# Attention reciprocals copied by VectorE shuffles instead of through DRAM, with larger rings in the expert weights' memory

## The chip, the cores and the metric

The kernel runs on one core of one Trainium2 chip. The metric is the device time of one launch in microseconds (us). The kernel before takes 1158.88 us, the median of 3 runs (1156.53 to 1162.4).

## The reference, cut to what matters

`x` is 8 batches of 1024 rows of 128. The block is attention with an adjacency mask, then a mixture of 8 experts.

```python
# attention, after a layer norm of x; H = 4 heads of 32, Nc = 8 chunks of 128 keys
scores = einsum('bhnd,bhjcd->bhnjc', q, kc) / sqrt(32)
scores = clip(scores, -10, 10);  scores = where(mask == 0, -10, scores)
attn = softmax(scores, axis=-1)          # over the 128 keys of one chunk
ctx = einsum('bhnjc,bhjcd->bhnd', attn, vc)
out = layernorm(ctx @ Wo.T + bo + x) * gamma + beta
# experts, after a layer norm: top 2 of 8 by a softmax gate
h = gelu(xf @ w1 + bb1);  y = h @ w2 + bb2;  acc = acc + we[:, None] * y   # for each expert
```

The softmax is over each chunk alone. So every query has 8 denominators a head, one a chunk, and the part of the context from each chunk is multiplied by its own reciprocal before the chunks are added.

## The kernel before, in words

**Attention.** A batch is 16 steps (`STEPS`): 2 halves of 512 queries by 8 chunks of keys. In a step PE computes `scores` of two heads twice (u = 0, 1; L1123), VectorE clips and masks them (`clip`, L822), ScalarE takes the exponential (L621), PE multiplies by `v` (`contexts`, two steps later, L1137) and adds up the denominators (`denominators`, L1150). ScalarE copies the context of the step from PSUM to the ring `ctx_sb` (`ctx_copy`, L597; `RING` = 8 places), and GpSimd multiplies it by `rspread` and adds it to the sum of its half (`normalise`, L408 to L416), `LAG` = 9 steps behind in its list. Between these stand the projections of the next batch and the output projection and layer norm of the last (`post_...`). Each engine has its list in a fixed order, and all waiting is by semaphores.

**The reciprocals.** The denominators of 4 steps (`GROUP`) and 4 heads lie in one PSUM tile of 128 rows by 256: in the 32 rows of a head, row 2j + c holds step j of the group, queries c x 256 to c x 256 + 255. VectorE inverts it once in 4 steps into `rinv` (`invert`, L833). GpSimd needs, for each step, the 512 reciprocals of a head in all its 32 partitions. `spread` on SP's queue makes that copy: it stores `rinv` in DRAM (L335, 128 KB), waits until it has landed, and loads it back with each row repeated over 32 partitions (L341, two transfers of 512 KB, each for two steps). `rspread` has 4 places, and each of the two transfers waits until GpSimd has used the places before (`chunk_added`). The next batch's Q and K go through DRAM on ScalarE's queue (`qk_dram`, then `qstack` and `kstack`, L570 and L583).

**The rest.** SP's list runs in order. It loads x of batch 0, weights, x of batches 1 to 3, and the adjacency; after the mask is made, the expert weights W1 and W2 (L322, L324), into the place of x of batches 4 to 7; and, behind the first `spread` and the split of the weights, x of batches 4 to 7 (`load_x(2)`). VectorE takes the statistics of these in steps 9 to 13 of batch 0 (L795). GpSimd splits W1 and W2 into high and low halves (`split_ffn`, L456 to L460) at the start. After attention VectorE takes statistics of all rows (L946), the gate follows, and from about 755 us the experts: `hidden`, gelu, `second`, with GpSimd at L507.

Of the kernel before, what the change touches and what calls it, by code (L numbers as in the profile page):

```python
# [24 lines left out]
ACT = mybir.ActivationFunctionType  # L25
# [7 lines left out]
P = 128  # L33
# [9 lines left out]
def gnn_moe(nc, x, adj, Wq, bq, Wk, bk, Wv, bv, Wo, bo, gamma, beta, gate_w, gate_b, W1, b1, W2, b2, out):  # L43
# [19 lines left out]
    with ctx:  # L63
# [37 lines left out]
        w_raw = [x1[:, NB - 4 + 2 * i:NB - 2 + 2 * i, :].rearrange("p b n -> p (b n)") for i in range(2)]  # L101
# [16 lines left out]
        rspread = sb("rspread", [P, GROUP, HALF], F32)  # L118
# [15 lines left out]
        hid = ctx_sb[:, :, :].rearrange("p (r k) n -> p r k n", k=KH)  # L134
# [43 lines left out]
        den_dram = nc.dram_tensor("den_dram", (2, P, HALF // 2), F32, kind="Internal").ap()  # L178
# [44 lines left out]
        rinv_stored = sem("rinv_stored")  # L223
        rspread_loaded = [sem(f"rspread_loaded{j}") for j in range(GROUP)]
# [74 lines left out]
        def _(sp):  # L299
# [21 lines left out]
            sp.wait_ge(mask_made, T)  # L321
            sp.dma_start(w_raw[0].rearrange("p (e h) -> p e h", e=E),  # L322
# [3 lines left out]

            def spread(b, i, pairs=range(GROUP // 2)):

                G = GROUPS * b + i
                if pairs[0] == 0:  # L330
                    sp.wait_ge(rinv_ready, G + 1)


                    wait(sp, rspread_loaded[GROUP // 2 - 1], 16 * (G - 1))
                    sp.dma_start(den_dram[i % 2], rinv[:]).then_inc(rinv_stored, 16)  # L335
                    sp.wait_ge(rinv_stored, 16 * G + 16)
                rows = den_dram[i % 2].rearrange("(h m i r) q -> h m i (r q)", h=HEADS, i=GROUP // 2, r=GROUP)
                for j in pairs:

                    wait(sp, chunk_added, GROUP * (G - 1) + 2 * j + 2)  # L340
                    sp.dma_start(rspread[:, 2 * j:2 * j + 2, :],  # L341
                                 rows[:, 0, j:j + 1, :].to_broadcast([HEADS, DH, 2 * HALF])
                                 ).then_inc(rspread_loaded[j], 16)

            def body(b, par=None):
                par = b % 2 if par is None else par
                first, last = isinstance(b, int) and b == 0, isinstance(b, int) and b == LAST
                if not first:
                    spread(b - 1, GROUPS - 1)
                spread(b, 0)  # L350
                if first:

                    sp.wait_ge(ffn_step, 6)
                    load_x(2)
                spread(b, 1)
                spread(b, 2)

            batches(body)
            spread(LAST, GROUPS - 1)

# [12 lines left out]
        def _(pool):  # L373
# [24 lines left out]
            def normalise(b, s):  # L398
# [4 lines left out]
                pool.wait_ge(rspread_loaded[s % GROUP // 2], 16 * (GROUPS * b + s // GROUP + 1))  # L403
                fresh, by = ctx_sb[:, s % RING, :], rspread[:, s % GROUP, :]
# [57 lines left out]
            def body(b, par=None):  # L462
# [3 lines left out]
                for s in range(STEPS):  # L466
                    if s == 0 and not first and not second:
                        post_root(2 * b - 3)
                    if s == 12 and not first:
                        post_root(2 * b - 2)  # L470
                    if s >= LAG:
                        normalise(b, s - LAG)
                    elif not first:
                        normalise(b - 1, s - LAG + STEPS)
                    if s == 5 and not first and not second:
                        post_final(b - 2, 1)
                    if s == 14 and not first:
# [3 lines left out]
                    if s == 0 and first:  # L481
                        split_ffn(0, w1_hi[:, :, :].rearrange("p e h -> p (e h)"),
                                  w1_lo[:, :, :].rearrange("p e h -> p (e h)"))
                    if s == 4 and first:
                        split_ffn(1, w2_hi[:, :, :, :].rearrange("p e k d -> p (e k d)"),
                                  w2_lo[:, :, :, :].rearrange("p e k d -> p (e k d)"))
# [13 lines left out]
            post_final(LAST, 1)  # L500

# [16 lines left out]
        def _(act):  # L518
# [72 lines left out]
            def ctx_copy(b, s):  # L591
# [5 lines left out]
                act.activation(ctx_sb[:, s % RING, :], sum_ps[:, s % 2, :], ACT.Copy).then_inc(ctx_copied, 1)  # L597
# [143 lines left out]
        def _(dve):  # L741
# [85 lines left out]
            def invert(b, i):  # L827
# [57 lines left out]
            def body(b, par=None):  # L885
# [512 lines left out]
```

## Time and profile before

| | |
|---|---|
| median of 3 runs | 1158.88 us |
| the profiled execution | 1162.74 us, span 1160.9 us |
| PE busy | 921.1 us, 79% |
| VectorE busy | 773.1 us, 67% |
| ScalarE busy | 613.8 us, 53% |
| GpSimd busy | 713.5 us, 61% |
| transfers for `rspread` | 64 of 512 KB |
| transfers for `den_dram` | 32 of 128 KB |

The span is the time from the first to the last instruction in the profile; the execution's own time is 1.84 us longer. DVE is VectorE, ACT ScalarE, POOL GpSimd, and SPq and ACTq are the queues that issue transfers. Busy time doesn't count waiting, so a share says nothing by itself of what sets the end; the waits and the chain do.

### The profile page before, as it was taken

What the parts mean: (1) busy time and instruction counts of PE and PEld (TensorE: products, weight loads), DVE (VectorE), ACT (ScalarE), POOL (GpSimd) and SP (SyncE); (2) the same over time, 40 slices, a digit from 0 to 9 for tenths busy, and PEclk for the clock granted to TensorE, in tenths of its full rate; (3) what the DMA queues carried; (4) which work ended last, traced back from release to release, by engine and by line L of the source; (5) the groups of instructions that cost most, each with busy time, mean ns of one, the idle gap of its engine ahead of it and who ended that gap; (6) DMA issues with size and microseconds to landing.
All of it is one profiled execution on the core that took longest, in us unless ns stands there. A gap on an engine that the chain in (4) does not pass through costs nothing.

```text
span 1160.9 us, 23125 instructions
## 1 busy us (share of the span) xinstructions
PE 921.1 (79%) x8456; PEld 450.0 (39%) x8456; DVE 773.1 (67%) x1763; ACT 613.8 (53%) x948; POOL 713.5 (61%) x637
## 2 busy tenths in 40 slices
PE   4582797997877969879689407199999899899997
PEld 2221132231222313212222106056666666666665
DVE  5563897776765838758577386866666566566665
ACT  4561586756747658477566415154444344444443
POOL 2512455666656666667476860057787677777776
PEclk9595899898988979989899755589999999999999
DMA  8544426243262432433522210000000000000000
GB/s 283 132 95 103 106 84 145 73 130 99 84 139 75 130 102 79 120 100 97 134 66 76 77 42 1 0 2 11 19 11 11 12 10 11 21 10 11 10 11 20
DMA packets 42375, 79.59 MB, mean 69 GB/s; under 512 B 3196, under 2 KB 18455, under 8 KB 42263
## 3 DMA queue, kind: packets, MB, share of 16 engines
q1 hardware_dynamic: 28438, 52.92, 14.8%
q10 hardware_dynamic: 13824, 25.17, 9.3%
q8 instruction: 71, 1.16, 0.4%
q14 instruction: 42, 0.34, 0.1%
HBM read 61.30 MB, written 16.78 MB: 67 GB/s over the span
## 4 chain that ended last, share of the span: by engine, by line
DMA 31%; POOL 28%; issue 15%; PE 14%; DVE 9%; ACT 2%; POOLq 1%; ACTq 1%; SPq 1%; DVEq 0%
DMA rspread<-den_dram 14%; POOL prob_ring L507 14%; DMA den_dram<-rinv 9%; POOL ctx_sb L411 5%; POOL ctx_acc L416 4%; DMA x<-in_x 3%; DMA kstack<-qk_dram 2%; PE score_ps L1123 2%; DMA qk_dram<-qk_lo 2%; PE sum_ps L1137 2%; PE side_ps L1150 1%; POOL ctxT L416 1%; POOL x L442 1%; PE sum_ps L1319 1%; DVE limit L946 1%
## 5 line engine op out<-in xcount | busy, mean ns | idle before, releaser
L822 DVE SCALAR_TENSOR_TENSOR prob_ring<-score_ps,limit 128x1024 f32<-128x1024 f32 x256 | 305.7, 1212 | 123.2 <-PE score_ps L1123 122.6
L507 POOL TENSOR_TENSOR prob_ring<-ctx_sb,prob_ring 128x512 f16<-128x512 f32 x256 | 305.5, 1213 | 118.2 <-DVE prob_ring L1013 118.2
L621 ACT ACTIVATE prob_ring<-prob_ring 128x1024 f32<-128x1024 f32 x256 | 262.7, 1052 | 127.3 <-DVE prob_ring L822 97.3
L696 ACT ACTIVATE ctx_sb<-score_ps,vec 128x512 f32<-128x512 f32 x256 | 166.9, 684 | 171.4 <-PE score_ps L1085 171.4
L411 POOL TENSOR_TENSOR ctx_sb<-ctx_sb,rspread 128x512 f32<-128x512 f32 x112 | 142.9, 1276 | 157.4 <-DMA rspread<-den_dram 145.2
L1023 DVE SCALAR_TENSOR_TENSOR prob_ring<-sum_ps,cw_s,prob_ring 128x128 f32<-128x128 f32 x512 | 144.1, 344 | 136.7 <-PE sum_ps L1321 136.7
L1123 PE MATMUL score_ps<-qstack,kstack 128*128 128x512 f16 x512 | 168.4, 414 | 74.4 <-DVE prob_ring L822 38.1
L1319 PE MATMUL sum_ps<-w_hi,prob_ring 128*128 128x128 f16 x1024 | 180.3, 221 | 14.4 <-POOL prob_ring L507 12.3
L1320 PE MATMUL sum_ps<-w_lo,prob_ring 128*128 128x128 f16 x1024 | 179.5, 220 | 0.0
L1321 PE MATMUL sum_ps<-w_hi,prob_ring 128*128 128x128 f16 x1024 | 179.4, 220 | 0.0
L1137 PE MATMUL sum_ps<-prob_ring,v_sb 128*32 128x512 f32 x1024 | 152.0, 668 | 31.9 <-ACT ctx_sb L597 31.9
L1150 PE MATMUL side_ps<-prob_ring,gather 128*32 128x256 f32 x2048 | 142.9, 398 | 0.0
L1123 PEld LDWEIGHTS score_ps<-qstack,kstack 128*128 128x128 f16 x512 | 29.8, 99 | 252.7 <-issue 113.7
L416 POOL TENSOR_TENSOR ctx_acc<-ctx_acc,ctx_sb 128x512 f32<-128x512 f32 x96 | 122.4, 1275 | 7.5
L597 ACT ACTIVATE ctx_sb<-sum_ps 128x512 f32<-128x512 f32 x128 | 75.3, 589 | 95.7 <-POOL ctx_acc L416 63.8
L1319 PEld LDWEIGHTS sum_ps<-w_hi,prob_ring 128*128 128x128 f16 x1024 | 100.5, 98 | 50.4 <-POOL prob_ring L507 31.1
L1013 DVE CAST prob_ring<-ctx_sb 128x512 f16<-128x512 f32 x256 | 111.2, 475 | 4.8 <-issue 2.7
L1083 PE MATMUL score_ps<-qstack,w_hi 128*128 (+1 forms) x256 | 99.1, 387 | 7.6 <-issue 5.8
L1320 PEld LDWEIGHTS sum_ps<-w_lo,prob_ring 128*128 128x128 f16 x1024 | 100.8, 98 | 4.2 <-issue 0.6
L1321 PEld LDWEIGHTS sum_ps<-w_hi,prob_ring 128*128 128x128 f16 x1024 | 100.8, 98 | 0.0
L1085 PE MATMUL score_ps<-qstack,w_lo 128*128 (+1 forms) x256 | 99.3, 388 | 0.0
L1084 PE MATMUL score_ps<-kstack,w_hi 128*128 (+1 forms) x256 | 99.2, 388 | 0.0
(138 smaller groups left out, 1001.8 us busy)
## 6 DMA issues: line engine op xcount, KB each, us to landing
rspread<-den_dram SPq DMA_DIRECT2D x64, 512.0 KB
qstack<-qk_dram ACTq DMA_DIRECT2D x32, 256.0 KB, 7.9
kstack<-qk_dram ACTq DMA_DIRECT2D x32, 256.0 KB, 6.8
qk_dram<-qk_hi ACTq DMA_DIRECT2D x16, 256.0 KB, 5.0
qk_dram<-qk_lo ACTq DMA_DIRECT2D x16, 256.0 KB, 9.9
den_dram<-rinv SPq DMA_DIRECT2D x32, 128.0 KB, 8.4
out_x<-prob_ring SPq DMA_DIRECT2D x16, 256.0 KB, 2.3
x<-in_adj SPq DMA_DIRECT2D x4, 512.0 KB, 7.7
```

The lines of the kernel that those rows point to most:

```text
L411: pool.tensor_tensor(fresh, fresh, by, ALU.mult).then_inc(scaled_ready, 1)
L416: pool.tensor_tensor(ctxT[:, half, :] if k == T - 1 else ctx_acc[:], ctx_acc[:], fresh, ALU.add).then_inc(chunk_added, 1)
L507: pool.tensor_tensor(hid_lo[:, u % 4, k, :], hid[:, u % 4, k, :], hid_hi[:, u % 4, k, :], ALU.subtract).then_inc(hid_lo_ready, 1)
L621: act.activation(probs[:, s % 4, 2 * u:2 * u + 2, :], probs[:, s % 4, 2 * u:2 * u + 2, :], ACT.Exp, scale=1.0 / SCORE).then_inc(exp_done, 1)
L696: act.activation(hid[:, u % 4, k, :], score_ps[:, 2 * (u % 2) + k, :], ACT.Gelu, bias=vec[:, KH * u + k:KH * u + k + 1], scale=1.0 / WSCAL ...
L822: dve.scalar_tensor_tensor(out=probs[:, s % 4, 2 * u:2 * u + 2, :], in0=score_ps[:, 2 * u:2 * u + 2, :], scalar=-LIMIT * SCORE, in1=limit[ ...
L1123: ins = pe.matmul(score_ps[:, h, :], kstack[:, par, h, k * P:k * P + P], qstack[:, par, h, half * HALF:half * HALF + HALF], start=True, st ...
L1137: ins = pe.matmul(sum_ps[head, s % 2, :], v_sb[:, par, k, head], probs[:, s % 4, h, :], start=True, stop=True, tile_position=(0, DH * h))
L1150: ins = pe.matmul(den_ps[DH * h:DH * h + DH, :], gather[:, c, j, :], probs[:, s % 4, h, c * (HALF // 2):(c + 1) * (HALF // 2)], start=(j = ...
L1319: pe.matmul(dst, hi, w2_hi[:, u, k, :], start=(k == 0), stop=False)
L1320: pe.matmul(dst, hi, w2_lo[:, u, k, :], start=False, stop=False)
L1321: ins = pe.matmul(dst, lo, w2_hi[:, u, k, :], start=False, stop=(k == KH - 1))
```

## The change

VectorE itself copies the reciprocals. A shuffle (`stream_shuffle`) takes, in every group of 32 partitions, the row that a mask names for each of the 32; with one row named 32 times it is a broadcast. Two shuffles of 128 x 256 a step replace SP's transfers. `rspread` has 8 places, `ctx_sb` 12 (`RING`), and `LAG` is 8. For the room, the split expert weights lie in the second halves of these rings, so they are loaded and split after attention, and raw weights in `prob_ring`. `load_x(2)` stands where the weights' load was.

```diff
-    RING = 2 * GROUP
+    RING = 3 * GROUP
-    LAG = GROUP + 5
+    LAG = GROUP + 4
-        rspread = sb("rspread", [P, GROUP, HALF], F32)
+        rspread = sb("rspread", [P, 2 * GROUP, HALF], F32)
+        w1_hi, w1_lo = [rspread[:, GROUP + 2 * i:GROUP + 2 * i + 2, :]...
+        w2_hi, w2_lo = [ctx_sb[:, 2 * GROUP + 2 * i:2 * GROUP + 2 * i + 2, :]...
+        w_raw = [clip_buf[:, E * HID * i:E * HID * (i + 1)] for i in range(2)]
...
             sp.wait_ge(mask_made, T)
+            load_x(2)
+
+            sp.wait_ge(ctx_done, STEPS * NB)
+            sp.wait_ge(den_added, STEPS * NB)
             sp.dma_start(w_raw[0]...
-            def spread(b, i, pairs=range(GROUP // 2)):
...
+                pool.wait_ge(rspread_ready, g + 1)
+                fresh, by = ctx_sb[:, g % RING, :], rspread[:, s % (2 * GROUP), :]
...
-                wait(dve, rinv_stored, 16 * G)
+                wait(dve, rspread_ready, GROUP * G)
                 dve.reciprocal(rinv[:], den_ps).then_inc(rinv_ready, 1)
+            def spread(b, s):
+                g, j = STEPS * b + s, s % GROUP
+                if j == 0:
+                    dve.wait_ge(rinv_ready, g // GROUP + 1)
+                wait(dve, chunk_added, g - 2 * GROUP + 1)
+                for c in range(2):
+                    ins = dve.stream_shuffle(rspread[:, s % (2 * GROUP), c * (HALF // 2):(c + 1) * (HALF // 2)], rinv[:],
+                                             [2 * j + c] * DH)
+                ins.then_inc(rspread_ready, 1)
...
                     clip(b, s, 1)
+                    if s >= GROUP + 2:
+                        spread(b, s - GROUP - 2)
+                    elif not first:
+                        spread(b - 1, s - GROUP - 2 + STEPS)
```

GpSimd's `split_ffn` moves from steps 0 and 4 of batch 0 behind its last `post_final`, and PE waits for it just before the first `hidden`.

VectorE's list at steps 14 and 15 of a batch, before (`prob_ring<-score_ps,limit` is a clip, `rinv` the reciprocal):

```order
L822 SCALAR_TENSOR_TENSOR prob_ring<-score_ps,limit 128x1024 [waits den_added,ctx_done,qk_done]
L833 RECIPROCAL rinv<-side_ps 128x256 [waits rinv_stored,den_added]
L822 SCALAR_TENSOR_TENSOR prob_ring<-score_ps,limit 128x1024 [waits qk_done]
L822 SCALAR_TENSOR_TENSOR prob_ring<-score_ps,limit 128x1024 [waits den_added,ctx_done,qk_done]
L856 BN_AGGR moments<-stats 128x2 [waits shift2_ready,stats2_done]
```

And with the change:

```order
L786 SCALAR_TENSOR_TENSOR prob_ring<-score_ps,limit 128x1024 [waits den_added,ctx_done,qk_done]
L797 RECIPROCAL rinv<-side_ps 128x256 [waits rspread_ready,den_added]
L786 SCALAR_TENSOR_TENSOR prob_ring<-score_ps,limit 128x1024 [waits qk_done]
L807 STREAM_SHUFFLE rspread<-rinv 128x256 [waits chunk_added,rinv_ready]
L807 STREAM_SHUFFLE rspread<-rinv 128x256
L786 SCALAR_TENSOR_TENSOR prob_ring<-score_ps,limit 128x1024 [waits den_added,ctx_done,qk_done]
L832 BN_AGGR moments<-stats 128x2 [waits shift2_ready,stats2_done]
```

Two shuffles stand between the second clip of a step and the first of the next; only the first of a pair has waits.

SP's list after the small loads, before:

```order
L322 DMA x<-in_L_ffn_W 128x8x256 [waits mask_made]
L324 DMA x<-in_L_ffn_W 128x16x128
L335 DMA den_dram<-rinv 128x256 [waits rinv_ready]
L341 DMA rspread<-den_dram 128x1x1024 [waits rinv_stored]
L341 DMA rspread<-den_dram 128x1x1024
L302 DMA x<-in_x 128x32x128 [waits ffn_step]
```

And with the change:

```order
L300 DMA x<-in_x 128x32x128 [waits mask_made]
L324 DMA prob_ring<-in_L_ffn_W 128x8x256 [waits den_added,ctx_done]
L326 DMA prob_ring<-in_L_ffn_W 128x16x128
```

All of x is asked for once the mask is made, and the expert weights after attention.

GpSimd's list at the end of attention, with the change (`x<-res,x` is the last `post_final`; before, the experts' L507 follows it at once):

```order
L410 TENSOR_TENSOR x<-res,x 128x512 [waits y_scaled]
L424 TENSOR_SCALAR prob_ring<-prob_ring 128x2048 [waits ffn_w_loaded]
L426 TENSOR_SCALAR rspread<-prob_ring 128x2048 [waits ffn_step]
L428 TENSOR_TENSOR rspread<-prob_ring,rspread 128x2048 [waits ffn_step]
L424 TENSOR_SCALAR prob_ring<-prob_ring 128x2048 [waits ffn_w_loaded]
L426 TENSOR_SCALAR ctx_sb<-prob_ring 128x2048 [waits ffn_step]
L428 TENSOR_TENSOR ctx_sb<-prob_ring,ctx_sb 128x2048 [waits ffn_step]
L471 TENSOR_TENSOR prob_ring<-ctx_sb,prob_ring 128x512 [waits hid_hi_ready] x32
```

The six operations of the split now stand between attention and the experts.

## Rows read from the trace of the kernel before

**Rows 1.** The page: the chain's shares by engine, and the spreading transfers.

```profile
DMA 31%; POOL 28%; issue 15%; PE 14%; DVE 9%; ACT 2%; POOLq 1%; ACTq 1%; SPq 1%; DVEq 0%
DMA rspread<-den_dram 14%; POOL prob_ring L507 14%; DMA den_dram<-rinv 9%; POOL ctx_sb L411 5%; POOL ctx_acc L416 4%; DMA x<-in_x 3%; DMA kstack<-qk_dram 2%; PE score_ps L1123 2%; DMA qk_dram<-qk_lo 2%; PE sum_ps L1137 2%; PE side_ps L1150 1%; POOL ctxT L416 1%; POOL x L442 1%; PE sum_ps L1319 1%; DVE limit L946 1%
...
rspread<-den_dram SPq DMA_DIRECT2D x64, 512.0 KB
```

**Rows 2.** Waits, 146.81 to 590.93 us: total, times, longest.

```profile
POOL ctx_sb L411 <- DMA rspread<-den_dram: 101.3, 24, 6.9
DVE prob_ring L822 <- PE score_ps L1123: 93.6, 81, 7.5
...
PEld score_ps L1123 <- DMA kstack<-qk_dram: 32.0, 6, 7.2
```

**Rows 3.** The chain in order of time, batch 5: start, us, what.

```profile
443.61 8.46 DMA den_dram<-rinv
452.09 8.76 DMA rspread<-den_dram
...
475.02 16.64 DMA den_dram<-rinv
491.68 12.84 DMA rspread<-den_dram
```

**Rows 4.** VectorE's timeline: start, us, instruction, idle before it and releaser.

```profile
105.86 1.65 DVE L795 BATCH_NORM_STATS2 stats<-x 128x6 f32<-128x128 f32 x8 [26.15 <-DMA x<-in_x]
...
146.81 1.75 DVE L833 RECIPROCAL rinv<-side_ps 128x256 f32<-128x256 f32 x1
...
590.93 1.75 DVE L833 RECIPROCAL rinv<-side_ps 128x256 f32<-128x256 f32 x1
...
646.95 1.23 DVE L822 SCALAR_TENSOR_TENSOR prob_ring<-score_ps,limit 128x1024 f32<-128x1024 f32 x1 [3.72 <-PE score_ps L1123]
```

**Rows 5.** Busy time by stretch: PE, PEld, DVE, ACT, POOL; clock, DMA, GB/s.

```profile
358.00:434.00 76.00, 63.14 (x520) 19.85 (x512) 52.10 (x61) 49.97 (x73) 48.98 (x44) 0.90 0.37 105
...
sum 304.00, PE 250.59 PEld 77.54 DVE 206.40 ACT 199.43 POOL 193.75; mean PE 62.65 PEld 19.39 DVE 51.60 ACT 49.86 POOL 48.44
```

**Rows 6.** PE's timeline, two `scores` pairs on.

```profile
143.48 0.60 PE L1123 MATMUL score_ps<-qstack,kstack 128*128 128x512 f16 x2
...
146.56 0.60 PE L1123 MATMUL score_ps<-qstack,kstack 128*128 128x512 f16 x2
```

**Rows 7.** The chain behind attention: short VectorE instructions, and the last spreading.

```profile
661.10 7.09 DMA rspread<-den_dram
668.21 10.94 DVE limit L946 x56
...
729.10 3.91 DVE limit L980 x56
733.03 7.71 DVE limit L984 x57
```

**Rows 8.** VectorE: L757 twice in the timeline; durations of L848, min/median/max.

```profile
679.92 1.26 DVE L757 TENSOR_SCALAR mean<-mean 128x56 f32<-128x56 f32 x1
...
745.54 0.16 DVE L757 TENSOR_SCALAR mean<-mean 128x8 f32<-128x8 f32 x1
...
L848 DVE BATCH_NORM_STATS2 stats<-res x64: 274/277/295, 173.0 to 714.6; 128x6 f32<-128x128 f32 x64
```

**Rows 9.** SP's timeline; landing times of L324 (W2) and of L302 (x).

```profile
73.15 0.76 SPq L302 DMA_DIRECT2D x<-in_x  x1
...
DMA to landing us min/median/max: 11.5/11.5/11.5
...
DMA to landing us min/median/max: 4.4/8.2/32.7
```

**Rows 10.** Timeline: GpSimd's split and its last row before the experts; VectorE then.

```profile
40.32 1.90 POOL L458 TENSOR_SCALAR w_hi<-x 128x2048 f16<-128x2048 f32 x1
42.31 4.06 POOL L460 TENSOR_TENSOR w_lo<-x,w_hi 128x2048 f16<-128x2048 f32 x1
...
730.27 1.26 POOL L442 TENSOR_TENSOR x<-res,x 128x512 f32<-128x512 f32 x1
...
741.02 1.16 DVE L990 TENSOR_TENSOR limit<-expert_no,limit 128x448 f32<-128x448 f32 x2
```

More of the change, by code:

```diff
@@ L99, in gnn_moe @@
             [ctx_sb[:, 2 * t:2 * t + 2, :].rearrange("p r n -> p (r n)").bitcast(I32) for t in range(T - 4)]
-        w_raw = [x1[:, NB - 4 + 2 * i:NB - 2 + 2 * i, :].rearrange("p b n -> p (b n)") for i in range(2)]
         xn = sb("xn", [P, 3, T, P], F32)
@@ L117, in gnn_moe @@
         rinv = sb("rinv", [P, HALF // 2], F32)
-        rspread = sb("rspread", [P, GROUP, HALF], F32)
+        rspread = sb("rspread", [P, 2 * GROUP, HALF], F32)
+        w1_hi, w1_lo = [rspread[:, GROUP + 2 * i:GROUP + 2 * i + 2, :].rearrange("p r n -> p (r n)").bitcast(F16)
+                        .rearrange("p (e h) -> p e h", e=E) for i in range(2)]
+        w2_hi, w2_lo = [ctx_sb[:, 2 * GROUP + 2 * i:2 * GROUP + 2 * i + 2, :].rearrange("p r n -> p (r n)").bitcast(F16)
+                        .rearrange("p (e k d) -> p e k d", e=E, k=KH) for i in range(2)]
+        w_raw = [clip_buf[:, E * HID * i:E * HID * (i + 1)] for i in range(2)]
         ctx_acc = sb("ctx_acc", [P, HALF], F32)
@@ L222, in gnn_moe @@
         rinv_ready = sem("rinv_ready")
-        rinv_stored = sem("rinv_stored")
-        rspread_loaded = [sem(f"rspread_loaded{j}") for j in range(GROUP)]
+        rspread_ready = sem("rspread_ready")
         scaled_ready = sem("scaled_ready")
@@ L325, in _ @@
                          W2.rearrange("e (k p) d -> p e k d", p=P)).then_inc(ffn_w_loaded, 16)
-            def spread(b, i, pairs=range(GROUP // 2)):
[L329 to L359, printed above, removed]
             def store(b, half):
@@ L480, in body @@
                         add_beta(b + 1)
[L481 to L486, printed above, removed]
             batches(body)
@@ L500, in _ @@
             post_final(LAST, 1)
+            split_ffn(0, w1_hi.rearrange("p e h -> p (e h)"), w1_lo.rearrange("p e h -> p (e h)"))
+            split_ffn(1, w2_hi.rearrange("p e k d -> p (e k d)"), w2_lo.rearrange("p e k d -> p (e k d)"))
             def hid_low(c, u):
@@ L596, in ctx_copy @@
                 wait(act, chunk_added, g - RING + 1)
-                act.activation(ctx_sb[:, s % RING, :], sum_ps[:, s % 2, :], ACT.Copy).then_inc(ctx_copied, 1)
+                act.activation(ctx_sb[:, g % RING, :], sum_ps[:, s % 2, :], ACT.Copy).then_inc(ctx_copied, 1)
             act.wait_ge(w_split, 5)
@@ L920, in _ @@
             batches(body)
+            spread(LAST, STEPS - GROUP - 2)
+            spread(LAST, STEPS - GROUP - 1)
             invert(LAST, GROUPS - 1)
+            for j in range(GROUP):
+                spread(LAST, STEPS - GROUP + j)
             post_res(LAST, 0)
@@ L1353, in _ @@
             pe.wait_ge(res_ready, 2 * NB)
+            pe.wait_ge(ffn_step, 6)
             hidden(0, 0)
```

10 lines of the change are left out of this document (1 added, 9 removed).

## The prediction

> **What bounds the kernel now.** I read the chain that ended last first. Transfers are its largest part [rows 1], and two thirds of them are the way of the reciprocals through DRAM (23% of the span). The other large entry, GpSimd at L507, is the expert stage after 755 us, where nothing is edited. So attention, up to about 650 us, is the place.
>
> Next the waits of attention [rows 2]. GpSimd waits 101 us at L411 for `rspread`, and in consequence VectorE waits 94 us for scores: `ctx_copy` on ScalarE finds no ring place, PE no free `sum_ps`. The third row is a second transfer, `kstack` (32 us in 6 waits, about 5 us a batch).
>
> The chain in one batch [rows 3] shows why: one storing of `rinv` and one spreading take 8.5 + 8.8 us when the queues are free and 16.6 + 12.8 when they carry `qk_dram` too. That is longer than four steps, and the rings of 8 copies and 4 reciprocals hold no more.
>
> How long a batch takes: the reciprocal of step 2 of batch 1 starts at 146.81, that of batch 7 at 590.93 [rows 4]; 444.1 us for 6 batches, 74.0 each. In 304 us of this stretch (4.1 batches) VectorE is busy 206.4 [rows 5], so 206.4 / 304 x 74.0 = 50.2 a batch. PE's own pace stands where nothing is late: two `scores` pairs, with what lies between, take 146.56 - 143.48 = 3.08 us [rows 6], a step. Sixteen are 49.3 us, without the next batch's projections and the output projections. With all of it PE is busy 250.59 / 304 x 74.0 = 61.0 a batch [rows 5], a part of it at the lower clock level (granted 0.90 in one of these stretches); at the full clock I estimate 58. Both engines could be done in 61; the reciprocals' way costs the rest.
>
> **The change, part by part.** The sum is made against the profiled execution: span 1160.9, time 1162.74. The median of the runs is 1158.88, so the forecast is that median plus the sum.
>
> *The price of a shuffle.* The trace has none. Each is two instructions, a load of the mask and the shuffle of 256 elements. Nearest rows [rows 7]: 56 BN_STATS of 128 elements take 10.94 us, 0.195 each; 56 MAX8 of 8 elements 3.91, 0.070 each; so 120 elements more cost 0.125, 1.04 ns an element. The pairs of L984, a value load and a search of 8 elements, take 7.71 / 56 = 0.138. A pair with 256 elements is then 0.138 + 248 x 1.04 ns = 0.40; I take 0.42. Low end 0.33, when the load is hidden. High end 0.53, when neither instruction overlaps its neighbours.
>
> The Trainium skill, VectorE: DVE Perf Modes, section "The perf-mode tier table", gives a STREAM_SHUFFLE of 2048 elements about 2400 ns with one program, at one element a cycle. An estimate from it for 256 is 2400 - 1792 / 0.96 = 533 ns, at my high end; by it the sum below would be 26 us smaller. No run before the change shows one.
>
> *Batches 1 to 6.* 32 shuffles are 13.4 us; VectorE then has 50.2 + 13.4 = 63.6 a batch against PE's 58 and becomes the bound. VectorE is no longer ahead, so a wait of a neighbour for it can't be made up: PE's output projections sit in two steps, and `qk_lo` follows ScalarE. I add 3.4 and get 67.0. Both transfers' waits go: GpSimd's because a shuffle is behind the reciprocal by a clip only, `kstack`'s because eight spreadings of 512 KB a batch leave the queues [rows 1]. 6 x (74.0 - 67.0) = -42. Bounds: 62 (no coupling, 0.33) to 72 (0.53 and 5 of coupling).
>
> *What the moved rows make wait.* Each pair stands behind the second clip and before the next step's first clip. Its wait is for a chunk of 7 steps earlier, with 8 reciprocal places, so GpSimd must be 8 steps late to stop it. `ctx_copy` on ScalarE has 12 places and GpSimd follows by 8. I cost both at nothing; the cover is some 4 steps, about 16 us. What is late next is VectorE itself.
>
> *Batch 0.* `load_x(2)` is issued at 73.15 behind the first spreading, lands 32.7 us later, and VectorE stands 26.2 us before the statistics of 105.86 [rows 4, 9]. In the change it is issued at about 26, where the expert weights' load was, and even at 32.7 us lands by 59; -26.2. Twelve shuffle pairs come in before step 2 of batch 1: at most 10.1. In plain steps VectorE has 3.08 - 2 x 1.23 = 0.62 idle [rows 4, 6], against 0.84 for a pair. With the statistics in between half is left: +5.
>
> *The start.* `load_x(2)` (2 MB in rows of 512 bytes) takes the place of 2 MB in rows of 1 KB and 512 bytes, which landed in 11.5 us [rows 9], beside the stacking of batch 0 for which the first scores wait. +2 (0 to +8).
>
> *Batch 7.* No next batch to prepare. Between step 2 and the last clip (590.93 to 648.18) 57.3 us pass; with 13.5 steps at 3.9, 53: -4.
>
> *From the last clip to the statistics of the expert stage.* Now 668.21 - 648.18 = 20.0, of which 7.1 the last spreading [rows 4, 7]. Afterwards: PE's last contexts and denominators 4, reciprocal 1.75, four shuffle pairs 3.4, residual and its statistics 2: 11. GpSimd's way (post_root, then five operations of 1.28, post_final 2.6) is about as long. -9.
>
> *The shared port.* Among the small operations of L752 to L784 behind the statistics of 668.21, that of L757 takes 1.26 us, and 0.16 when it comes back at 745.54 [rows 8]; ten of them take over 1.1 us, while GpSimd is still normalising. When GpSimd ends some 26 us after the last clip and they start at 22, about four are held instead of ten: -6.
>
> *The split.* Six operations of GpSimd, 1.90 + 1.90 + 4.06 twice [rows 10], move behind its last row at 730.27. They run from 731.5 to 747.6, and PE needs the weights some 7 us later; the load of 2 MB after the last denominator (11.5 us) is long there. Hidden, but for the port: VectorE is at two-input rows from 741.0 on [rows 10] and may get one through per operation of GpSimd until 747.6. +6 (0 to +10).
>
> The sum: -42 - 26.2 + 5 + 2 - 4 - 9 - 6 + 6 = -74. 1158.9 - 74 = 1085. As each of the small gains can only come whole, I say 1087.
>
> **The rivals.**
>
> *The shuffles wait for GpSimd (slower).* Place: every shuffle in batches 0 to 7. L757 is a one-input operation in SBUF and still waited out a GpSimd operation. GpSimd is busy 193.75 of 304 us [rows 5], 0.64, and with batches of 67 us 0.72. At 0.72 x about 1.0 us each, 256 shuffles cost 184 us more on the bounding engine: 1087 + 184 = 1271. It decides from 0.73 us a shuffle on (0.42 + 74 / 240). Against it: 64 BN_STATS of L848, also one input in SBUF, all took 274 to 295 ns while GpSimd was as busy [rows 8]. The question is to which kind a shuffle belongs. The Trainium skill, SBUF — State Buffer, section "SBUF: two separate sides", has only VectorE operations in a two-port mode or with two SBUF inputs contend; by it, and by the shuffle's single program, the trace's split between these two rows is explained and a shuffle is free. 7%.
>
> *Dear shuffles or more coupling.* A drained mask load, 0.55 each, and 5 of coupling: 50.2 + 17.6 + 5 = 73 a batch, no gain there; 1085 + 36 + 6 = 1127. For: nothing shows what a load of the mask waits for. 12%.
>
> *`kstack` remains.* ScalarE stands for a store of its own before it issues the stacking; if that is latency and not traffic, 5 us a batch stay: 1087 + 30 = 1117. For: the row of 32 us [rows 2]. Against: the chain's transfers double when two kinds meet [rows 3]. 8%.
>
> *PE bounds.* Shuffles at 0.33 fall into waits that VectorE had anyway: 62 a batch, 1087 - 30 = 1057. For: in plain steps 0.62 is idle. Against: 50.2 + 10.6 are already 61. 12%.
>
> *The path is not what it seems, no difference.* 1%.
>
> **How the numbers follow.** The forecast holds 60%, with its own range 1065 to 1110 (a shuffle 0.09 lower or 0.11 higher by 240 is -22 or +26). The cheap side takes the range to 1055, the dear one and `kstack` to 1125. The slower rival lies outside; below 1055 and above 1125 are left about 15%. A difference of 0.5% (6 us) is what a measurement of this kernel can tell from none. Faster 0.91, same 0.02, slower 0.07.
>
> **What would show it.** Right: STREAM_SHUFFLE rows of 0.3 to 0.45 us whose length doesn't depend on GpSimd; reciprocals of step 2 some 67 us apart; VectorE over 90% busy there, PE's wait for it; no wait for `rspread` on GpSimd nor for `kstack` on PE; no gap before the statistics of batches 4 to 7; some 11 us from the last clip to the 56 BN_STATS of the expert stage. Wrong: shuffles over 0.6 us; a gap of VectorE before the first scores that grew by over 8 us; the first matmul of the experts waiting for GpSimd's split. The whole falls if batches still take over 73 us.

## The result and the profile after

The changed kernel takes 1045.41 us (median of 4 runs, 1044.61 to 1047.92) against 1157.7 us before on the same chip: a ratio of 0.903, 95% interval 0.900 to 0.906. That is 112 us less, where the forecast had 72 and its range ended at 1055. The profiled execution has a span of 1043.1 us (time 1044.94), 117.8 less than the span of before. The page's chain by engine, its row of memory traffic, its groups of the shuffle and of the scores, and two of its transfers:

```profile
DVE 35%; issue 23%; POOL 19%; PE 17%; ACT 2%; DMA 2%; ACTq 1%; POOLq 0%; DVEq 0%
...
HBM read 27.74 MB, written 12.58 MB: 39 GB/s over the span
...
L1107 PE MATMUL score_ps<-qstack,kstack 128*128 128x512 f16 x512 | 158.1, 391 | 43.2 <-DVE prob_ring L786 32.9
...
L807 DVE STREAM_SHUFFLE rspread<-rinv 128x256 f32<-128x256 f32 x256 | 102.0, 451 | 0.0
...
kstack<-qk_dram ACTq DMA_DIRECT2D x32, 256.0 KB, 4.8
...
qk_dram<-qk_lo ACTq DMA_DIRECT2D x16, 256.0 KB, 3.7
```

Transfers were 31% of the chain [rows 1] and are 2%; VectorE went from 9% to 35%. Attention is where the time went. Three stretches of it by engine (PE, PEld, DVE, ACT, POOL busy, granted clock, share of the DMA engines, GB/s), against [rows 5]:

```profile
160.00:220.00 60.00, 57.34 (x510) 18.03 (x507) 59.93 (x120) 49.73 (x72) 48.60 (x42) 1.00 0.19 48
280.00:340.00 60.00, 57.54 (x512) 18.32 (x510) 59.93 (x121) 49.31 (x71) 48.77 (x43) 1.00 0.18 49
400.00:460.00 60.00, 57.10 (x504) 17.72 (x501) 59.93 (x125) 50.39 (x72) 47.79 (x43) 1.00 0.19 48
```

VectorE is busy 59.93 of 60 us: it is the bound, with nothing lost between its instructions. PE follows at 57.3 of 60, and its granted clock is 1.00, the level of 2.4 GHz throughout, where a stretch of before had 0.90, a mean of the two levels [rows 5]. The waits from 160 to 460 us (total, times, longest), against [rows 2]:

```profile
PEld score_ps L1107 <- DVE prob_ring L786: 89.7, 112, 1.6
...
POOL ctx_sb L379 <- DVE rspread L807: 18.3, 15, 2.3
...
PE score_ps L1107 <- DVE prob_ring L786: 13.5, 38, 0.7
```

No transfer is waited for any more, and VectorE waits for nobody. What waits for the clips are PE's weight loads (PEld), 89.7 us in total and at most 1.6 at a time, for the most part while earlier matmuls still run: the matmuls themselves wait 13.5 us. How far apart the batches are and how a shuffle stands among VectorE's other work (start, us), against [rows 4]:

```profile
122.51 1.75 DVE L797 RECIPROCAL rinv<-side_ps 128x256 f32<-128x256 f32 x1
...
487.01 0.01 DVE L807 LOAD_MASK_SELECT rspread<-rinv  x1
487.01 0.45 DVE L807 STREAM_SHUFFLE rspread<-rinv 128x256 f32<-128x256 f32 x1
487.36 0.01 DVE L807 LOAD_MASK_SELECT rspread<-rinv  x1
487.36 0.45 DVE L807 STREAM_SHUFFLE rspread<-rinv 128x256 f32<-128x256 f32 x1
487.71 1.21 DVE L786 SCALAR_TENSOR_TENSOR prob_ring<-score_ps,limit 128x1024 f32<-128x1024 f32 x1
488.83 1.75 DVE L797 RECIPROCAL rinv<-side_ps 128x256 f32<-128x256 f32 x1
```

The first and last row are the reciprocals of step 2 of batches 1 and 7: (488.83 - 122.51) / 6 = 61.05 us a batch, 74.0 before. The next instruction starts 0.35 us after a shuffle (487.01, 487.36, 487.71), though the shuffle's record is 0.45 long: records overlap, and the distance to the next start is the price. Added up from start to start over the batch from 366.71 on, the 32 shuffles take 11.0 us and all other work of VectorE 50.0, the 50.2 of the prediction, with no wait between them. The 256 shuffles take 0.424 to 0.493 us, none 1 us, with GpSimd busy for 48 of 60 us beside them. The mask's load has a record of 0.01 us and the shuffle starts with it: it is hidden.

The stretch behind attention, against [rows 4, 7, 8, 10]:

```profile
537.19 1.20 DVE L786 SCALAR_TENSOR_TENSOR prob_ring<-score_ps,limit 128x1024 f32<-128x1024 f32 x1
...
549.11 1.07 DVE L930 BATCH_NORM_STATS2 limit<-x 128x6 f32<-128x128 f32 x5
...
564.32 1.16 DVE L728 TENSOR_SCALAR var_e<-var_e 128x56 f32<-128x56 f32 x1
565.51 0.19 DVE L731 TENSOR_SCALAR rstd<-var_e 128x56 int32<-128x56 int32 x1
...
569.41 0.86 DVE L918 TENSOR_SCALAR xn<-x,mean,rstd 128x128 f32<-128x128 f32 x3
...
617.41 6.74 DVE L974 TENSOR_TENSOR limit<-expert_no,limit 128x448 f32<-128x448 f32 x2
```

From the last clip to the statistics 10.7 us pass (538.39 to 549.11), 20.0 before. Five of the small operations that follow are held by GpSimd instead of ten. The row at 617.41 took 1.16 before and now meets GpSimd's split of the expert weights (607.40 to 623.68). The first matmul of the experts starts at 636.3.

### The profile page after: what moved, and what is told of

The parts are those of the page before. It is cut to its first block, busy times and chain, and to the rows that moved or that the text cites. A ratio compares the mean times of both kernels' runs of the same rounds, so it can differ in the third digit from the quotient of the medians.

```text
span 1043.1 us, 23507 instructions
## 1 busy us (share of the span) xinstructions
PE 887.6 (85%) x8456; PEld 441.6 (42%) x8456; DVE 845.3 (81%) x2275; ACT 617.4 (59%) x948; POOL 715.3 (69%) x637
## 3 DMA queue, kind: packets, MB, share of 16 engines
q8 instruction: 71, 1.16, 0.5%
## 4 chain that ended last, share of the span: by engine, by line
DVE 35%; issue 23%; POOL 19%; PE 17%; ACT 2%; DMA 2%; ACTq 1%; POOLq 0%; DVEq 0%
POOL prob_ring L471 15%; DVE prob_ring L786 13%; DVE rspread L807 7%; DVE rinv L797 4%; PE score_ps L1107 3%; PE sum_ps L1121 2%; PE side_ps L1134 2%; DMA kstack<-qk_dram 1%; PE sum_ps L1303 1%; DVE qk_lo L775 1%; PE score_ps L1067 1%; DVE limit L930 1%; POOL ctx_sb L379 1%; PE sum_ps L1305 1%; PE sum_ps L1304 1%
## 5 line engine op out<-in xcount | busy, mean ns | idle before, releaser
L585 ACT ACTIVATE prob_ring<-prob_ring 128x1024 f32<-128x1024 f32 x256 | 268.3, 1055 | 107.6 <-DVE prob_ring L786 95.8
L786 DVE SCALAR_TENSOR_TENSOR prob_ring<-score_ps,limit 128x1024 f32<-128x1024 f32 x256 | 306.0, 1206 | 15.0 <-PE score_ps L1107 14.6
L1107 PE MATMUL score_ps<-qstack,kstack 128*128 128x512 f16 x512 | 158.1, 391 | 43.2 <-DVE prob_ring L786 32.9
L1303 PE MATMUL sum_ps<-ctx_sb,prob_ring 128*128 128x128 f16 x1024 | 180.2, 221 | 14.4 <-POOL prob_ring L471 12.5
L1304 PE MATMUL sum_ps<-ctx_sb,prob_ring 128*128 128x128 f16 x1024 | 179.4, 220 | 0.0
L1305 PE MATMUL sum_ps<-ctx_sb,prob_ring 128*128 128x128 f16 x1024 | 179.2, 220 | 0.0
L1121 PE MATMUL sum_ps<-prob_ring,v_sb 128*32 128x512 f32 x1024 | 138.1, 611 | 0.2 <-ACT ctx_sb L561 0.2
L1134 PE MATMUL side_ps<-prob_ring,gather 128*32 128x256 f32 x2048 | 137.0, 385 | 0.0
L1303 PEld LDWEIGHTS sum_ps<-ctx_sb,prob_ring 128*128 128x128 f16 x1024 | 100.5, 98 | 50.4 <-POOL prob_ring L471 31.0
L1067 PE MATMUL score_ps<-qstack,rspread 128*128 (+1 forms) x256 | 99.0, 387 | 7.8 <-issue 6.1
L1304 PEld LDWEIGHTS sum_ps<-ctx_sb,prob_ring 128*128 128x128 f16 x1024 | 100.7, 98 | 4.3 <-issue 0.5
L807 DVE STREAM_SHUFFLE rspread<-rinv 128x256 f32<-128x256 f32 x256 | 102.0, 451 | 0.0
L1305 PEld LDWEIGHTS sum_ps<-ctx_sb,prob_ring 128*128 128x128 f16 x1024 | 100.7, 98 | 0.0
L1068 PE MATMUL score_ps<-kstack,rspread 128*128 (+1 forms) x256 | 99.3, 388 | 0.0
L1069 PE MATMUL score_ps<-qstack,rspread 128*128 (+1 forms) x256 | 99.3, 388 | 0.0
```

Source lines behind the costliest of these rows:

```text
L585: act.activation(probs[:, s % 4, 2 * u:2 * u + 2, :], probs[:, s % 4, 2 * u:2 * u + 2, :], ACT.Exp, scale=1.0 / SCORE).then_inc(exp_done, 1)
L786: dve.scalar_tensor_tensor(out=probs[:, s % 4, 2 * u:2 * u + 2, :], in0=score_ps[:, 2 * u:2 * u + 2, :], scalar=-LIMIT * SCORE, in1=limit[ ...
L807: ins = dve.stream_shuffle(rspread[:, s % (2 * GROUP), c * (HALF // 2):(c + 1) * (HALF // 2)], rinv[:], [2 * j + c] * DH)
L1107: ins = pe.matmul(score_ps[:, h, :], kstack[:, par, h, k * P:k * P + P], qstack[:, par, h, half * HALF:half * HALF + HALF], start=True, st ...
L1121: ins = pe.matmul(sum_ps[head, s % 2, :], v_sb[:, par, k, head], probs[:, s % 4, h, :], start=True, stop=True, tile_position=(0, DH * h))
L1134: ins = pe.matmul(den_ps[DH * h:DH * h + DH, :], gather[:, c, j, :], probs[:, s % 4, h, c * (HALF // 2):(c + 1) * (HALF // 2)], start=(j = ...
```

## The experiments

In all of them "batch" is the distance of the same two reciprocals divided by 6. Ratios are to the kernel before on the same chip, with their 95% interval; the changed kernel run once more beside some of them gave 1044.89 us, 0.903 (0.901 to 0.906):

> The changed kernel once more, on the chip of the three beside it: 1045 (1043 to 1048).

### Rings and transport taken apart

*Shuffles alone.* The two rings go back to 8 and 4 places:

```
-ctx_sb[:, g % RING, :], rspread[:, s % (2 * GROUP), :]     # RING = 12
+ctx_sb[:, g % (2 * GROUP), :], rspread[:, s % GROUP, :]
...
-wait(dve, chunk_added, g - 2 * GROUP + 1)
+wait(dve, chunk_added, g - GROUP + 1)
```

> The shuffles with the rings of before: 8 copies of contexts, 4 places of reciprocals; the loads as in the changed kernel. Theory (VectorE bounds attention at its own work, 50.2 us a batch and 32 shuffles of 0.345): a shuffle's place is free by then, since GpSimd scales a step right behind its shuffle; batches stay at 61.1 us and the time at 1045 (1043 to 1052). Rival (the larger rings brought the gain): copies or shuffles wait for a place again, batches of 65 us and over, 1070 and over.

Measured: 1048.87 us, 0.907 (0.903 to 0.910), batch 61.04. Attention is as in the changed kernel: the last reciprocal starts at 542.32, there at 542.42. The 3.5 us more are lost behind it: the first matmul of the experts starts at 639.6, 3.3 later. VectorE in this kernel:

```profile
546.43 0.01 DVE L807 LOAD_MASK_SELECT rspread<-rinv  x1 [0.83 <-POOL ctx_acc L384]
...
551.55 0.01 DVE L807 LOAD_MASK_SELECT rspread<-rinv  x1 [4.34 <-POOL ctx_acc L384]
```

The shuffles of the last four steps come at once, find no place (they wait for GpSimd's sums, which set places free), and the last residual stands behind them on VectorE. The larger rings are worth this tail and nothing else. By the wait it is the ring of reciprocals that counts; the last kernel below, with 8 places for copies and 8 for reciprocals, bears that out.

*Rings alone.* Through DRAM as before, with rings of 12 and 8 places and the new order of loads:

```
+for j in range(2): wait(sp, rspread_loaded[2 * o + j], 16 * (G // 2))
+sp.dma_start(den_dram[o], rinv[:])
...
+wait(sp, chunk_added, GROUP * (G - 2) + 2 * j + 2)
+sp.dma_start(rspread[:, GROUP * o + 2 * j:GROUP * o + 2 * j + 2, :], rows[...])
```

> The reciprocals through DRAM as before, with the larger rings (12 copies, 8 places), the early load of x and the late one of the weights. Theory (the transfers' latency and traffic held the batches up, and the rings hide a part only): VectorE has 50 us of work a batch, PE some 58; four storings, each waited for on the queue, take 34 to 66 us a batch by the rows of before. I expect 64 a batch and the last spreading back behind the last clip: 1045 + 6 x 3 + 9 = 1072 (1055 to 1110). Rival (the rings brought the gain, the shuffles only cost VectorE 11 us a batch): batches of 58 to 60, 1040 to 1050. Rival (rings are worth nothing without shuffles): 74 a batch, 1130.

Measured: 1103.98 us, 0.953 (0.949 to 0.957), batch 69.60, where 64 and 1072 us were expected (the time is still in the range). Its waits, 160 to 580 us:

```profile
POOL ctx_sb L399 <- DMA rspread<-den_dram: 89.8, 25, 9.2
...
PEld score_ps L1107 <- DMA kstack<-qk_dram: 48.5, 6, 9.8
```

The transfers are still waited for, and as the batches come closer `kstack` is later: up to 9.8 us, 7.2 before [rows 2]. With the same 61.30 MB read, the landing's median is 8.0 us; it was 6.8 before and is 4.8 in the changed kernel. This kernel differs from the changed one in the way of the reciprocals alone (and in `LAG`, 9 against 8), so that wait hangs on the traffic of the spreadings, as the prediction had it.

*The order of loads alone*, through DRAM and with the old rings:

> The order of loads alone: the reciprocals through DRAM and the rings of before, x of batches 4 to 7 loaded early, the expert weights after the last denominators and split by GpSimd behind its last normalisation. Theory: batches 1 to 6 stay at 74, batch 0 is shorter by 26 to 100 - 26 = 74, the expert stage starts 6 us later behind the split: 1158 - 26 + 6 = 1138 (1128 to 1148). Rival (an early load of x clears the queues and the batches themselves get shorter): batches under 72, below 1126.

Measured: 1139.29 us, 0.985 (0.981 to 0.989), batch 73.49: as the theory said. The order of loads is worth 17 us of the whole gain.

These three and the changed kernel give a table of two by two, all with the new order of loads (`LAG` is 9 in the upper row and 8 in the lower, which no run takes apart):

| | rings 8 and 4 | rings 12 and 8 |
|---|---|---|
| through DRAM | 1139.3 (73.49) | 1104.0 (69.60) |
| shuffles | 1048.9 (61.04) | 1045.4 (61.05) |

The rings are worth 35 us with the transfers and 3.5 with the shuffles; the shuffles 90 us with the old rings and 59 with the new. The two cure the same wait, so their gains can't be added.

### The price of a shuffle and the coupling of two nearly equal engines

Four kernels change the number or the width of the shuffles; a fifth lies between. Three of them, with one, with one and a half and with the narrow shuffle, leave a part of the reciprocals uncopied from the third group of steps on, so they don't compute the block; every wait and semaphore stays, and their times tell what the shuffles cost.

```
-for c in range(2):                            # changed kernel
+for c in range(2 if g < 2 * GROUP else 1):    # one shuffle a step
+for c in range(2 if g < 2 * GROUP else 2 - s % 2):    # three in two steps
+    ... rinv[:, 0:8] ...                      # one of 8 elements
...
+dve.stream_shuffle(spare[:, s % 2, :], rinv[:], [2 * j] * DH)    # a third one
...
+for c in range(4): ... rinv[:, c % 2 * 128:c % 2 * 128 + 128]    # four of 128
```

> From the third group of steps on only one of a step's two shuffles is issued: the reciprocals of the second half of a step's queries are not copied there, so 16 shuffles a batch instead of 32. Theory (VectorE's own work bounds: 50.2 us a batch and 0.345 for each shuffle): VectorE needs 55.7 a batch, PE about 58 and becomes the bound; 3 us less in each of 7 batches, 1045 - 21 = 1024 (1016 to 1030). Rival (VectorE doesn't bound, 61 us are PE's or GpSimd's): no change, 1045. Rival (each shuffle costs its whole record of 0.449 us or more, and nothing else bounds below): 61 - 7.2 = 54, 995.

> A third shuffle of 256 elements in every step, into a spare place that nobody reads. Theory: 16 x 0.345 = 5.5 us more in each of 7 to 8 batches, batches of 66.6 and 1045 + 7.6 x 5.5 = 1087 (1080 to 1094). Rival (the record's length of 0.449 us is the price): + 55, 1100. Rival (it falls into waits of VectorE): under 1060.

> Four shuffles of 128 elements in place of two of 256, with the same data. Tells the fixed part of a shuffle and its mask load from the part per element. Theory (1.04 ns an element, as in the rows of before, so 0.266 of 0.345 us, and 0.079 fixed): 64 x 0.212 = 13.6 us a batch instead of 11.0, + 2.5 a batch, 1045 + 19 = 1064 (1058 to 1070). Rival (mostly fixed: 0.3 us each): + 8 a batch, 1107. Rival (only elements count, the rest overlaps): 1045.

> From the third group of steps on one shuffle of 8 elements a step: the reciprocals are not copied there, but every wait and semaphore stays. It shows the floor without VectorE's extra work. Theory: VectorE has 50.2 + 16 x 0.09 = 51.6 us a batch and PE bounds at about 58; the time is that of the kernel with one shuffle a step within 3 us, 1024 (1016 to 1030). Rival (VectorE still bounds, by its waits for PE in each step): batches fall below 56 and the time below 1010. Rival (61 us a batch are not VectorE's): 1045.

> From the third group of steps on the second shuffle is issued in every other step, 24 shuffles a batch: the reciprocals of the second half of the queries of odd steps are not copied there. VectorE's own work is 50.2 + 24 x 0.345 = 58.5 a batch, PE's some 57.9: the point of balance. Theory (hardly any coupling, 0.5 at most): 59.0 a batch and 1045 - 6.9 x 2.1 = 1031 (1028 to 1034). Rival (coupling as forecast, up to 3.4 where both have the same work): 61.9 a batch, 1045 or more.

| shuffles a step | VectorE's own work a batch | batch | time (interval of the ratio) |
|---|---|---|---|
| one of 8 elements | | 57.42 | 1021.89 (0.876 to 0.884) |
| one | 50.2 + 5.5 = 55.7 | 58.20 | 1025.8 (0.880 to 0.888) |
| one and a half | 50.2 + 8.3 = 58.5 | 59.07 | 1031.53 (0.886 to 0.891) |
| two | 50.2 + 11.0 = 61.2 | 61.05 | 1045.41 (0.900 to 0.906) |
| four of 128 elements | 50.2 + 13.6 = 63.8 | 63.21 | 1062.17 (0.911 to 0.919) |
| three | 50.2 + 16.6 = 66.8 | 66.68 | 1086.7 (0.933 to 0.940) |

The column of own work is worked out: 50.2 and 0.345 a shuffle, and for the four narrower ones the 0.212 that was expected before the run. All five came out within their theory's range, only that the narrow one was to lie within 3 us of the kernel with one shuffle and lies 3.9 below it. The first row is PE's floor; its stretch from 160 us and that of the kernel with one and a half:

```profile
160.00:220.00 60.00, 59.89 (x540) 19.75 (x541) 53.91 (x96) 52.36 (x76) 51.19 (x47) 1.00 0.22 57
```

```profile
160.00:220.00 60.00, 58.86 (x526) 18.71 (x523) 59.38 (x112) 51.08 (x75) 49.60 (x44) 1.00 0.21 54
```

PE is busy 59.89 of 60 in the one; in the other PE has 58.86 and VectorE 59.38, the closest to balance, and the batch is 59.07, which is 0.6 above the larger of the two, 58.5. With one shuffle it is 0.8 above PE's 57.42. From 61 on a batch is VectorE's own work and nothing more: the three last rows measure 0.1 to 0.6 less than the column. The third shuffle costs (66.68 - 61.05) / 16 = 0.352 us. Halving the width gives (63.21 - 50.2) / 64 = 0.203 for 128 elements, against (61.05 - 50.2) / 32 = 0.339 for 256: about 1.06 ns an element and 0.07 us fixed.

### The split of the expert weights

Three kernels put GpSimd's six operations (1.9, 1.9 and 4.06 us, twice) elsewhere: ahead of the last root; one half between the last root and the last normalisation; or all behind VectorE's statistics.

```
+split_ffn(0, ...); split_ffn(1, ...)       # ahead of the root
 post_root(2 * LAST + 1)
...
+split_ffn(0, ...)                          # one half between
 post_final(LAST, 1)
...
-split_ffn(0, ...); split_ffn(1, ...)
+pool.wait_ge(b_shift_ready, 1)             # behind the statistics: this, the split, then the root
```

> The changed kernel, with GpSimd's split of the expert weights ahead of the last half of the last batch's root and normalisation, where GpSimd stands idle for some 25 us. Theory (the split made the first expert matmul 6 us late, by the port and by GpSimd itself): VectorE's residuals and statistics meet the split instead, at 1 to 4 us, and the expert stage starts 3 to 7 us earlier: 1040 (1037 to 1045). Rival (what came late there is PE's or VectorE's own chain, and the split lies beside it): 1045, within 2 us. Rival (the split ahead of the root holds VectorE's residual by its 4 us operations and the whole end is later): 1048 to 1055.

> The changed kernel, with GpSimd's split of W1 between the last root and the last normalisation, where GpSimd waits 11.8 us for ScalarE, and that of W2 behind the normalisation as now. What the earlier split showed: a small VectorE operation that meets the split lasts as long as the operation of GpSimd beside it (1.9, 2.0, 4.1 us). Theory: the split then ends by 615.5, ahead of VectorE's row of two inputs that took 6.7 us at 617.4 and takes 1.2 undisturbed; - 5.6, less what VectorE's four-tile rows lose between 593 and 601: 1041 (1038 to 1045). Rival (those rows are on the chain and are held by 4 us or more): 1045 and over.

> The changed kernel, with GpSimd's whole split behind a wait for VectorE's statistics of batches 0 to 6, so that it runs from about 569.5 to 585.5, in GpSimd's idle 24.5 us, beside VectorE's and ScalarE's normalisation of the expert stage. Theory: nothing small of VectorE stands there in a chain, the row at 617.4 is free, and what is lost is a few of the rows of tiles: 1042 (1039 to 1047). Rival (the rows of tiles and the residues from PSUM are held as well, each by the operation beside it, and PE waits for them in turn): 5 to 10 us lost for 5.6 won, 1047 to 1052.

Measured: 1051.96 (0.905 to 0.913), 1045.44 (0.902 to 0.906) and 1046.23 us (0.903 to 0.908). None gained: the first two missed their theories (1040 and 1041) and met a rival, the third lies 4 us above its theory's 1042, though within its range. Ahead of the root, GpSimd and then VectorE:

```profile
566.57 1.90 POOL L424 TENSOR_SCALAR prob_ring<-prob_ring 128x2048 f32<-128x2048 f32 x1
568.55 1.91 POOL L426 TENSOR_SCALAR rspread<-prob_ring 128x2048 f16<-128x2048 f32 x1
570.54 4.05 POOL L428 TENSOR_TENSOR rspread<-prob_ring,rspread 128x2048 f16<-128x2048 f32 x1
```

```profile
566.67 1.85 DVE L739 TENSOR_TENSOR msq<-rstd 128x56 f32<-128x56 f32 x1
568.56 1.96 DVE L741 SCALAR_TENSOR_TENSOR msq<-msq,var_e 128x56 f32<-128x56 f32 x1
570.55 4.11 DVE L744 SCALAR_TENSOR_TENSOR rstd<-msq,rstd 128x56 f32<-128x56 f32 x1
...
582.68 0.22 DVE L739 TENSOR_TENSOR msq<-rstd 128x56 f32<-128x56 f32 x1
```

Each operation of VectorE ends with the operation of GpSimd beside it; alone it takes 0.22. Six of them cost 14.5 us, the row of L974 gives 5.6 back, and the first matmul of the experts is 8.4 us later. The numbers came out as the last rival said, but at another victim than I had named: the statistics, not the residual. In the other two kernels the victims are the normalised tiles. Half between, then all behind the statistics:

```profile
594.91 6.53 DVE L918 TENSOR_SCALAR xn<-x,mean,rstd 128x128 f32 x4
```

```profile
573.86 0.68 DVE L926 TENSOR_TENSOR kstack<-sum_ps,qstack 128x512 f16<-128x512 f32 x1
575.15 6.89 DVE L919 TENSOR_SCALAR xn<-x,mean,rstd 128x128 f32<-128x128 f32 x4 [0.61 <-PE sum_ps L1064]
581.96 1.27 DVE L926 TENSOR_TENSOR kstack<-sum_ps,qstack 128x512 f16<-128x512 f32 x2
```

Four tiles take 1.1 us alone. The residue with one input in PSUM stays at 0.69 beside the split. The row of L974 is back at 1.16 in both kernels, but the tiles take back what it gives. In all three places VectorE had operations of the kinds that are held, with two inputs or a tensor-scalar and all in SBUF.

### The load of x

The load of x for batches 4 to 7 is held back, to the first reciprocal or to the first clip:

```
 sp.wait_ge(mask_made, T)
+sp.wait_ge(rinv_ready, 1)      # in the other kernel: sp.wait_ge(clip_done, 1)
 load_x(2)
```

> The changed kernel, with the load of x for batches 4 to 7 held back until the first reciprocal, about 71 us, its place before the change. Tells whether batch 0 lost its 26 us by the late issue or by the spreadings in the queues. Theory (both: the load landed 32.7 us after its issue among spreadings, and alone it lands in 14): landing by 85, before the statistics that are due at 80 to 90, a stall of under 5 us: 1046 (1044 to 1050). Rival (the issue's time alone): landing at 104 as before, + 20 us, 1065.

> The changed kernel, with the load of x for batches 4 to 7 held back until the first clip is done, some 44 us. Theory (only the 9 us of the first stacking's landing are hurt by a load beside them): as with the load at the first reciprocal, 1039 (1037 to 1041). Rival (a load beside batch 1's stores of queries and keys hurts as well): 1041 to 1045.

Measured: 1039.07 us, 0.898 (0.896 to 0.900), and 1040.15 us, 0.897 (0.895 to 0.900). I had expected no gain of the first; it was 6 us. The chain's stacking of batch 0 in the changed kernel (run once more) and with the load at the first reciprocal:

```profile
32.01 14.28 DMA kstack<-qk_dram
```

```profile
32.65 9.00 DMA kstack<-qk_dram
```

The first scores need this stacking, and 2 MB of x beside it cost it 5.3 us; the first clip is at 42.87 instead of 47.5. The load issued at 65.93 lands within 10.2 us and nobody waits for it. Before the change, issued at 73.15 behind a spreading, it took 32.7 [rows 9], and VectorE stood from 79.7 on [rows 4]. With 10.2 it would have landed at 83.4, so of that stall of 26 us some 22 were due to traffic and at most 4 to the time of its issue. With the load behind the first clip the time is the same, as expected.

### Put together

W2's parts get memory of their own, in place of the four additional places for context copies; W2 is loaded after the first clip and split at once, x is loaded behind that, and W1 alone is split at the end.

```
+    RING = 2 * GROUP
+    sp.wait_ge(clip_done, 1)
+    sp.dma_start(w_raw[1]..., W2...)      # w_raw[1] in x1 of batches 6 and 7
+    sp.wait_ge(ffn_step, 3)
     load_x(2)
```

> The changed kernel put together by what the runs so far say. The copies of contexts have 8 places again; W2's parts have memory of their own, W2 is loaded after the first clip (not beside the first stacking) and split by GpSimd before its first normalisation, when it stands idle for over 40 us and VectorE runs clips, residues from PSUM and shuffles; x of batches 4 to 7 is loaded behind that; W1 alone is loaded and split at the end, 8 us beside VectorE's MAX8 and index searches. Theory (the 5 us of the start and the 6 us of the split are apart and both avoidable): 1045 - 5.8 - 5.6 = 1034 (1031 to 1037). Rival (one of them comes back elsewhere, by VectorE's rows held in batch 0 or by GpSimd's late first normalisation): 1037 to 1042. Rival (the rings' missing places cost as in the kernel with small rings): 1037.

Measured: 1032.34 us (1030.88 to 1034.89), 0.890 (0.888 to 0.892); batch 61.06. GpSimd's last operation of the split and VectorE's row behind it:

```profile
606.85 4.06 POOL L430 TENSOR_TENSOR rspread<-prob_ring,rspread 128x2048 f16<-128x2048 f32 x1
```

```profile
612.39 1.16 DVE L977 TENSOR_TENSOR limit<-expert_no,limit 128x448 f32<-128x448 f32 x2
```

The split of W1 lies beside VectorE's MAX8 and index searches, which keep their lengths (56 MAX8 in 3.90 us, 3.91 before [rows 7]), and the row of two inputs is back at 1.16. That of W2 (50.32 to 58.40) lies beside clips, residues from PSUM and no other kind. The experts' first matmul starts at 625.7 instead of 636.3: 4.7 us by the start, the other 5.9 by the split. Neither comes back elsewhere, and the missing places of the copies cost nothing. Its slowest run (1034.89) is below the fastest of the changed kernel (1042.16) and of the two with a late load of x (1037.54).

## Why the prediction was wrong

The direction and the mechanism were right; the size was not. Its terms, and what the two profiled executions give:

| term | forecast | measured |
|---|---|---|
| batches 1 to 6 | -42 (67.0 each) | -77.8 (61.05 each) |
| start and batch 0, to the reciprocal of step 2 of batch 1 | -26.2 + 5 + 2 = -19.2 | 146.81 to 122.51: -24.3 |
| batch 7 | -4 | 57.3 to 49.6: -7.7 |
| last clip to statistics | -9 | 20.0 to 10.7: -9.3 |
| shared port: from there to the first tile of `xn` | -6 | 25.4 to 20.3: -5.1 |
| split: from there to the first matmul of the experts | +6 | 60.8 to 66.9: +6.1 |
| expert stage, to the end | 0 | 406.5 to 406.8: +0.3 |
| sum | -74, told as -72 | -117.8 |

**The step that failed** is "I add 3.4 and get 67.0". Of the 36 us missing in batches 1 to 6, 3.4 x 6 = 20 are this coupling. Measured, it is nothing at 61.2 to 57.4, and 0.6 to 0.8 us a batch where VectorE has 58.5 or 55.7. I argued that a wait of a neighbour for the bounding engine can't be made up. PE does wait (its matmuls 13.5 us in 300, its weight loads 89.7), but its waits cost only where they come back to VectorE as a wait for scores, and VectorE has none in these 300 us. That it is `score_ps` and the ring of probabilities between the two that keep them apart is my explanation; no run changed those buffers. There was no row for the 3.4; the rows gave both engines' work and so a bound, 50.2 + 13.4 = 63.6.

**The price of a shuffle** is the other part: 0.345 against the 0.42 chosen, 32 x 0.075 x 6 = 14 us, of which 0.02 a shuffle was my rounding up from 0.40. The measured value lies near the low end of 0.33 ("when the load is hidden"), and the load is hidden. The per-element slope from BN_STATS and MAX8 was right (1.04 against 1.06 ns). What was off was the fixed part, 0.13 us from pairs of a value load and a search, about twice the 0.07 of a mask load and a shuffle. The estimate of 533 ns by the Trainium skill, VectorE: DVE Perf Modes, section "The perf-mode tier table", is above the record (449) and further above the price (345); here the measurement decides.

**The range.** It was built around 67.0, and its low side ended at "PE bounds", 62 a batch and 1057. The two low ends, 0.33 a shuffle and no coupling, were written down as a bound of 62 (50.2 + 10.6 is 61) and then given 12% as a rival. It is what happened. Two small terms fell short by the same reasoning: batch 7 took 49.6 / 13.5 = 3.7 us a step, not 3.9, and the shuffles of batch 0, put at +5, cost 0.6: from the first clip to the reciprocal of 122.51 74.6 us pass, and before it was 100.2 less the stall of 26.2, 74.0.

**What held.** The waits named went away, `kstack`'s too, and the kernel with transfers and larger rings shows that it was traffic. The cover of the moved rows held in the batches; the small rings show where it ends, in the tail. The shuffles do not wait for GpSimd. The Trainium skill, SBUF — State Buffer, section "SBUF: two separate sides", had let a shuffle pass; the 256 records between 0.424 and 0.493 us agree. The three small terms of the end, -9, -6 and +6, came out within 1 us, but by luck in one case: I had taken the +6 for a price of the port as such, and the last kernel shows it avoidable. The start's +2 came out as +1.3, with a 2 MB load beside the first stacking in both kernels: that stacking took 12.5 us before and 14.6 after, and 9.0 without a load. Without one the start is 4.6 us shorter than the changed kernel's, which I did not ask. PE's work at the full clock, estimated at 58 a batch, is 58.2 in the changed kernel (286.2 in 300 us).

**Slips in the working,** none of which moves the forecast: the way of the reciprocals is 23 of 31% of the span, three quarters of the transfers and not two thirds; GpSimd's share in batches of 67 us is 0.70, not 0.72; and [rows 8] set 56 elements beside 8, where 56 alone take 0.18 (L721 of the changed kernel).

## What to carry to other kernels

- Where a wait goes and an engine becomes the bound, forecast its own work first, with nothing added: here the coupling was 0 when VectorE had 4 us a batch more than its neighbour, and 0.6 at balance. Any surcharge needs a row.
- An instruction's price on a full engine is the distance to the next start, not the record's length; here 0.345 against 0.449 us. Changing its count or width on the bounding engine measures it.
- Deeper buffers and shorter latency cure the same wait: 35 us and 90 us apart, 94 together. And before a gap is filled with a load or a GpSimd operation, ask what lies beside it: a bulk load cost the critical stacking 5 us, and the split was free only beside operations of VectorE that it didn't hold.

## What the runs showed of the hardware

- A VectorE operation that reads only SBUF (two inputs, or a tensor-scalar) and starts beside a GpSimd operation in most cases ended with it, whatever its own length: 0.22 us became 1.85, 1.96 and 4.11 beside operations of 1.90, 1.91 and 4.05. One that started at the same moment as GpSimd's (565.51 in the changed kernel) kept its 0.19. Shuffles, MAX8 (3.90 us for 56), BN_STATS (10.92 for 56) and operations with one input in PSUM (0.69) kept their lengths.
- TensorE's granted clock in attention: before, 0.90 from 358 to 434 us (PE busy 63.14 of 76) and 0.88 from 206 to 282 (68.03 of 76), means of the two levels; 1.00, the level of 2.4 GHz, in each 60 us from 160 to 460 of the changed kernel (57.1 to 57.5 busy) and of that with three shuffles a step (52.7 to 53.8). No run shows what it goes by.
- A STREAM_SHUFFLE of 256 f32 elements cost 0.345 us in a full queue, one of 128 some 0.20, with its mask load hidden; their records are 0.449 and 0.300 long (medians).
